# Moving the output spectra between two vector engines in a cross-attention and FFN kernel

## The reference

```python
q, k, v = LN(x) @ Wq.T + bq, ctx @ Wk.T + bk, ctx @ Wv.T + bv     # (4, 512, 16, 16)
corr = irfft(rfft(q) * conj(rfft(k))).mean(channels)              # (4, 16, 512)
weights, delays = top_k(corr, 6); w = softmax(weights)
out = sum_i w[i] * roll(v, delays[i]);  x = x + out @ Wo.T + bo
h = gelu(bitlinear(LN(x), w1, b1))                                # (4, 512, 1024)
x = x + bitlinear(h, w2, b2)
# bitlinear(x, w, b): y = rmsnorm(x); scale = 127 / max|y| per row; round(y * scale) / scale,
#                     w rounded to -1, 0, 1 times mean|w|; then a matrix product and the bias
```

## Time and profile before

| what | us |
|---|---|
| median of 3 runs | 181.0 |
| lowest and highest run | 180.97, 183.41 |
| the profiled execution | 182.84 |
| its span, first to last instruction | 180.8 |
| busy: TensorE, ScalarE, GpSimd | 159.7, 89.7, 83.9 |
| mean granted TensorE clock over the span, as a share of full speed | 0.98 |

### The profile page before, as it was taken

How to read it: one execution, slowest core, us unless ns; L and a number is a source line. 1 busy time by engine, 2 the same in 40 slices (tenths; PEclk the granted TensorE clock), 3 DMA queues, 4 the chain that set the end, 5 groups by cost and what they waited for, 6 DMA issues and landing times.

```text
span 180.8 us, 2886 instructions
## 1 busy us (share of the span) xinstructions
PE 159.7 (88%) x869; PEld 107.1 (59%) x877; DVE 149.8 (83%) x347; ACT 89.7 (50%) x158; POOL 83.9 (46%) x150
## 2 busy tenths in 40 slices
PE   7989889998999998999994977993799999999943
PEld 2635667657655956576873755670456766555632
DVE  1537299999299996999979999779997999999992
ACT  3136615548722441211510521519449999999821
POOL 6030899754440003932009827071985654454430
PEclk9999999999999999999999999999589999999999
DMA  5999989080474000000000001616447101111012
GB/s 191 319 289 391 359 289 190 3 116 0 64 107 61 5 0 0 0 0 5 2 0 0 0 0 29 91 29 87 64 59 115 58 29 58 44 45 62 29 58 87
DMA packets 14128, 15.07 MB, mean 83 GB/s; under 512 B 1186, under 2 KB 13347, under 8 KB 14116
## 3 DMA queue, kind: packets, MB, share of 16 engines
q1 hardware_dynamic: 9892, 10.73, 17.9%
q0 software_dynamic: 4224, 4.19, 15.8%
HBM read 8.61 MB, written 2.10 MB: 59 GB/s over the span
## 4 chain that ended last, share of the span: by engine, by line
PE 25%; DVE 24%; issue 7%; POOL 1%; DVEq 1%; ACT 0%; POOLq 0%
PE psum L469 4%; PE psum L458 4%; DVE c_f L1046 4%; PE psum L518 4%; PE psum L538 3%; DVE res L1061 2%; DVE hmax L1035 2%; DVE stats L910 2%; PE psum L520 2%; PE psum L338 2%; PE psum L529 2%; DVE prod_sum L763 1%; DVE xmax L924 1%; DVE m_b L884 1%; DVE out_f L891 1%
## 5 line engine op out<-in xcount | busy, mean ns | idle before, releaser
L390 PE MATMUL psum<-wkv,c_f 128*128 128x512 f32 x64 | 29.0, 598 | 0.8 <-ACT c_f L580 0.8
L1035 DVE TENSOR_REDUCE hmax<-wf 128x1 f32<-128x1025 f32 x16 | 19.4, 1211 | 0.7 <-ACT wf L683 0.7
L390 PEld LDWEIGHTS psum<-wkv,c_f 128*128 128x128 f32 x64 | 11.8, 190 | 13.7 <-issue 12.4
L683 ACT ACTIVATE wf<-psum,xdeq 128x1024 f32<-128x1024 f32 x16 | 17.6, 1101 | 1.3 <-PE psum L520 1.3
L599 ACT COPY kv_f<-psum 128x512 f32<-128x512 f32 x16 | 9.1, 582 | 18.4 <-PE psum L390 18.4
L691 ACT ACTIVATE x_f<-wf 128x1024 f32<-128x1024 f32 x16 | 16.9, 1056 | 0.0
L458 PE MATMUL psum<-to_signal,out_f 128*128 128x256 f32 x64 | 14.6, 382 | 2.4 <-POOL out_f L1170 2.4
L518 PE MATMUL psum<-w1q,xq_t 128*128 128x512 bf16 x59 | 16.2, 392 | 0.5 <-issue 0.3
L538 PE MATMUL psum<-w2q,kv_f 128*128 128x256 bf16 x128 | 16.4, 273 | 0.0
L469 PE MATMUL psum<-wo,out_t 128*128 128x256 f32 x64 | 14.9, 386 | 1.3 <-DVE out_t L898 1.3
L403 PE MATMUL psum<-wq,x_f 128*128 128x256 f32 x64 | 15.1, 381 | 0.8 <-ACT x_f L580 0.8
(11 more groups left out here) (164 smaller groups left out, 351.0 us busy)
## 6 DMA issues: line engine op xcount, KB each, us to landing
ctx_in<-in_ctx SPq DMA_DIRECT2D x4, 512.0 KB, 5.1
res<-in_x SPq DMA_DIRECT2D x4, 512.0 KB, 6.5
res<-bo_all POOLq DMA_DIRECT2D x4, 512.0 KB, 5.2
res<-b_all POOLq DMA_DIRECT2D x4, 512.0 KB, 5.9
out<-res SPq DMA_DIRECT2D x16, 128.0 KB, 1.7
wf<-in_w_t SPq DMA_DIRECT2D x1, 1024.0 KB, 8.3
wf<-in_w_t SPq DMA_DIRECT2D x2, 512.0 KB, 9.7
wkv<-in_wkv_t SPq DMA_DIRECT2D x1, 512.0 KB, 7.5
```

The lines of the kernel that those rows point to most:

```text
L390: mm = pe.matmul(bank(K_BANKS + ft), c_f[:, c, ft * P:(ft + 1) * P], wkv[:, c, :], start=(c == 0), stop=(c == NC - 1))
L683: act.activation(hid[j], hb, ACT.Gelu, scale=xdeq[:, m, j:j + 1]).then_inc(s["hid_made"], 1)
L1035: dve.tensor_reduce(hmax[:, j:j + 1], hid_and_least[j], AX.X, ALU.max, apply_absolute_value=True).then_inc(s["hmax_made"], 1)
```

## The change

- **Output spectra by batch.** GpSimd computes real and imaginary part of batches 0, 1 and 3 (`out_spectrum`, six instructions of 128x512 each, in place of three for every batch). VectorE computes batch 2 in two halves of heads (`out_spectrum_halves`, twelve instructions of 128x256), and TensorE may start half c = 0 once the first six are done. `out_f` becomes a pair of buffers.
- **Weights of the delays.** The comparison that made a mask (L835) goes; one instruction selects and sums; the scaling of a 32x512 tile becomes that of a 32x32 diagonal, by which TensorE's turn multiplies.
- **Rounding of x** goes from VectorE to ScalarE (`round_x`, four activations); VectorE gets a small multiplication for the scale (`x_scales`) and keeps the cast (`whole_x`).
- **PSUM banks.** Projection uses banks 4 and 5, the turns of x 2 and 3 (for batches 2 and 3: 6 and 7).
- **TensorE's order.** `up(0, 0)` goes between the halves of `inverse(3)`; the turns of batches 2 and 3 go to tiles 4 and 6.
- **Late norms between tiles.** On VectorE the residual, norm and maximum of batches 2 and 3 are spread over tiles 0 to 4, and ScalarE's and GpSimd's orders follow.

```diff
-                    pe.wait_ge(s["out_im_made"], n + 1)
+                if n == FIRST_LATE:
+                    pe.wait_ge(s["out_half_made"], 2 * c + 2)
+                elif c == 0:
...
             pe.wait_ge(s["consts"], 3)
-            for n in (2, 3):
-                inverse(n, 0)
-                inverse(n, 1)
-                keep_busy(M_BANKS[1], 5)
-                project(n, 0)
-                project(n, 1)
-                turn_x(n - 2)
 
             def up(m, j):
...
 
+            inverse(2, 0)
+            inverse(2, 1)
+            keep_busy(X_BANKS, 5)
+            project(2, 0)
+            project(2, 1)
+            turn_x(0)
+            inverse(3, 0)
             pe.wait_ge(s["w_quantised"], 2)
             pe.wait_ge(s["b1_made"], 16 * NPART)
+            up(0, 0)
+            inverse(3, 1)
+            keep_busy(X_BANKS, 5)
+            project(3, 0)
+            project(3, 1)
+            turn_x(1)
+            pe.wait_ge(s["xt_copied"], 4)
             for m in (0, 1):
                 for j in range(NA):
                     t = NA * m + j
+                    for n in X_TURNED:
+                        if t == X_TURNED[n] + 1:
+                            pe.wait_ge(s["xt_copied"], n * 2 + 2)
                     if t > TURNED:
                         turn_h(m, j)
-                    if t == 1:
-                        pe.wait_ge(s["at_used"], 4 * NB)
-                    up(m, j)
-                    if t == 1:
-                        turn_x(2)
+                    if t:
+                        up(m, j)
                     if t == 2:
...
 
+            def round_x(n):
+                act.wait_ge(s["xscale_made"], n + 1)
+                if n:
+                    act.wait_ge(s["xq_made"], n)
+                for a in range(NA):
+                    ins = act.activation(xround[:, a, :], xc[:, n % 2, a, :], ACT.Identity, scale=xscale[:, a:a + 1])
+                ins.then_inc(s["xround"], 1)
+
             def copy_x(n):
...
+            inverse_copy(3, 0)
+            gelu(0, 0)
+            inverse_copy(3, 1)
+            square(0, 0)
+            round_x(1)
+            centre(2)
+            copy_x(1)
             for m in (0, 1):
...
+                    for n in X_TURNED:
+                        if t == X_TURNED[n]:
+                            copy_x(n)
                     if t >= COPIED:
                         copy_h(m, j)
-                    if t == 0:
+                    if t:
+                        square(m, j)
+                    if t == 2:
                         centre(3)
-                    if t == 1:
-                        copy_x(2)
-                    square(m, j)
...
+            def weigh(g):
+
                 dve.wait_ge(s["rest_made"], g + 1)
-                dve.tensor_tensor(rest[:, 0:L], corr[:, 0:L], rest[:, 0:L], ALU.not_equal).then_inc(s["mask_made"], 1)
-
-            def weigh(g):
-
-                dve.wait_ge(s["mask_made"], g + 1)
                 dve.wait_ge(s["exp_made"], g + 1)
-                dve.tensor_tensor_reduce(out=expd[:], in0=expd[:], in1=rest[:, 0:L], scale=1.0, scalar=0.0,
-                                         op0=ALU.mult, op1=ALU.add, accum_out=gsum[:]).then_inc(s["gsum_made"], 1)
+                dve.scalar_tensor_tensor(chosen[:], rest[:, 0:L], TAKEN, expd[:], ALU.is_le, ALU.mult,
+                                         accum_out=gsum[:]).then_inc(s["gsum_made"], 1)
                 dve.wait_ge(s["gsum_made"], g + 1)
                 dve.reciprocal(grec[:], gsum[:]).then_inc(s["grec_made"], 1)
                 dve.wait_ge(s["grec_made"], g + 1)
-                dve.tensor_scalar(chosen[:], expd[:], grec[:, 0:1], None, ALU.mult).then_inc(s["g_made"], 1)
+                dve.tensor_scalar(g_diag[:], eye[0:GR, 0:GR], grec[:, 0:1], None, ALU.mult).then_inc(s["g_made"], 1)
...
+            def out_spectrum_halves(n):
+                dve.wait_ge(s["g_ready"], n // (NB // NG) * 3 + 3)
+                dve.wait_ge(s["at_done"], n * 4 - 6)
+                v = [by_heads(kv_f[:, n, part:part + 3:2, D:2 * D]) for part in range(2)]
+                g_r, g_i, g_x = [g[:, :, bass.ds(n * H, H)].unsqueeze(3).broadcast_to([P, 2, H, DK]) for g in (g_re, g_im, g_rx)]
+                m = [by_heads(m_halves[:, k]) for k in range(4)]
+                for c in range(NC):
+                    h = slice(c * H // NC, (c + 1) * H // NC)
+                    cols = slice(c * P, (c + 1) * P)
+                    dve.tensor_tensor(m[0][:, :, h], v[0][:, :, h], g_r[:, :, h], ALU.mult)
+                    dve.tensor_tensor(m[1][:, :, h], v[1][:, :, h], g_i[:, :, h], ALU.mult).then_inc(s["m_half_made"], 1)
+                    dve.tensor_tensor(m[2][:, :, h], v[1][:, :, h], g_x[:, :, h], ALU.mult)
+                    dve.tensor_tensor(m[3][:, :, h], v[0][:, :, h], g_i[:, :, h], ALU.mult).then_inc(s["m_half_made"], 1)
+                    dve.wait_ge(s["m_half_made"], 2 * c + 1)
+                    dve.tensor_tensor(out_f[:, n % 2, :, 0, cols], m_halves[:, 0, :, cols], m_halves[:, 1, :, cols],
+                                      ALU.subtract).then_inc(s["out_half_made"], 1)
+                    dve.wait_ge(s["m_half_made"], 2 * c + 2)
+                    dve.tensor_tensor(out_f[:, n % 2, :, 1, cols], m_halves[:, 2, :, cols], m_halves[:, 3, :, cols],
+                                      ALU.add).then_inc(s["out_half_made"], 1)
 
             def inverse_out(n, c):
...
             copy_g_spectrum(1)
-            out_re_products(2)
-            out_re(2)
+            out_spectrum_halves(FIRST_LATE)
...
                 inverse_out(n, 1)
-                if n + 1 < NB:
-                    out_re_products(n + 1)
-                    out_re(n + 1)
-                quantise_x(n - 2)
                 x_deq(n - 2)
-            add_residual(3, 0)
-            add_residual(3, 1)
-            stats2(3)
-            mean_var2(3)
-            row_max(2)
-            x_inverse(2)
-            quantise_x(2)
-            x_deq(2)
-
+                whole_x(n - 2)
...
-                    if (m, j) == (0, 0):
+                    if t == 0:
+                        add_residual(3, 0)
+                        add_residual(3, 1)
+                        row_max(2)
+                        x_scales(2)
+                        x_deq(2)
+                    if t == 1:
+                        stats2(3)
+                        mean_var2(3)
+                        whole_x(2)
+                    if t == 2:
                         row_max(3)
-                        x_inverse(3)
-                        quantise_x(3)
+                        x_scales(3)
                         x_deq(3)
+                    if t == 4:
+                        whole_x(3)
...
+                    pool.wait_ge(s["out_re_made"], by_pool(n) - 1)
+                    pool.wait_ge(s["out_im_made"], by_pool(n) - 1)
+                pool.tensor_tensor(by_heads(m_a[:]), v_of(n, 0), g_of(g_re, n), ALU.mult)
+                pool.tensor_tensor(by_heads(m_b[:]), v_of(n, 1), g_of(g_im, n), ALU.mult).then_inc(s["m_ab"], 1)
                 pool.tensor_tensor(by_heads(m_c[:]), v_of(n, 1), g_of(g_rx, n), ALU.mult)
                 pool.tensor_tensor(by_heads(m_d[:]), v_of(n, 0), g_of(g_im, n), ALU.mult).then_inc(s["m_cd"], 1)
-
-            def out_im(n):
-
-                pool.wait_ge(s["m_cd"], n + 1)
-                if n:
-                    pool.wait_ge(s["at_done"], n * 4 - 2)
-                pool.tensor_tensor(out_f[:, :, 1, :], m_c[:], m_d[:], ALU.add).then_inc(s["out_im_made"], 1)
+                if n > 1:
+                    pool.wait_ge(s["at_done"], n * 4 - 6)
+                pool.wait_ge(s["m_ab"], by_pool(n))
+                pool.tensor_tensor(out_f[:, n % 2, :, 0, :], m_a[:], m_b[:], ALU.subtract).then_inc(s["out_re_made"], 1)
+                pool.wait_ge(s["m_cd"], by_pool(n))
...
-            for n in (0, 1):
-                out_im_products(n)
-                out_im(n)
-            out_im_products(2)
-            out_im(2)
+            out_spectrum(0)
+            out_spectrum(1)
+            out_spectrum(3)
             x_rms(0)
-            out_im_products(3)
-            out_im(3)
             aug_parts(0)
             add_b2(0)
             x_rms(1)
             aug_parts(1)
             add_b2(1)
```

More of the change, by code:

```diff
@@ L1234, in _ @@
             add_b2(2)
+            h_deq(0, 1)
             x_rms(3)
[L1236 removed]
+            h_deq(0, 2)
+            add_b2(3)
+            h_deq(0, 3)
+            h_deq(1, 0)
             aug_parts(3)
[L1238 to L1242 removed]
+            for j in range(1, NA):
+                h_deq(1, j)
             with pool.Fori(2, NB) as m:
```

121 lines of the change are left out of this document (54 added, 67 removed).

## The result

The changed kernel takes **194.45 us** (median of 4, 192.32 to 195.92) against 181.45 of the kernel before on the same chip (lowest and highest 180.97 and 183.41): ratio 1.0615, 95% interval 1.0462 to 1.0769. That is slower, as forecast, but by 13 in place of 7.5 and outside the range. The profiled execution took 195.21. Page: span, and busy time by engine, against the earlier trace rows.

A forecast was written before the change was run, and what follows sets the result against it. Busy shares named no bound; TensorE's path was taken as longest up to T0, VectorE as pacing after it. Shifts of 2.2 and 5.3 on the 181.0 median gave 188.5 us, range 180 to 191.

The forecast's parts named there:

- Order of the work by turns: At the memory ports VectorE and GpSimd alternate; each waits for one whole instruction of the other, however short its own.
- Part 1: First group's spectra: cross spectra wait for GpSimd by turns, `correlate(1)` at about 84.0 instead of 81.77, T0 2.2 later.
- Part 1 and 2: Turns at the cross spectra, then at batch 2's halves beside batch 3: halves ready about 7.0 and 10.1 after T0.
- T0: Moment the second weights' spectrum is ready, 94.51 before the change; forecast to come 2.2 later.
- TensorE gains the 0.5 that it waited there: Before the first weights' spectrum: without GpSimd's bias row in VectorE's way, the spectrum is ready at 71.2 instead of 71.7.
- all unchanged: TensorE from `correlate(1)` to the second weights' spectrum: projection, inverse, turn and spectrum keep their lengths.
- Part 3: VectorE from T0 to tile 3: 40.7 of work plus 7.9 of waits, 48.6 in place of 43.3, 5.3 later.
- From there on its order per tile is untouched by the change, but for one cast of 0.3, so what follows keeps its length: VectorE from the hidden maximum of tile 3 (137.85 before) to the end: no change in length forecast.
- The moved turns of batches 2 and 3 lie behind VectorE's pace: TensorE's later turns of x: claimed not to hold VectorE up, so no time was added for them.
- VectorE keeping the ports, wholly or in part: Ports: GpSimd's turn comes only at the end (177.8, chance 0.16), or VectorE gets two turns for one (about 181, 0.14).
- That the clock costs nothing: Projection of batch 2: the clock holds or recovers in time, VectorE's wait shrinks by 2.6, giving 185.8; chance 0.20.
- Rivals 1 and 4: Clock costs nothing (185.8, chance 0.20); clock also falls before `correlate(1)`, costing TensorE up to 2.6 (190.9, chance 0.08).

The follow-up runs named there:

- b1: Kernel before with only the new output spectra by batch (batch 2 in halves on VectorE, the rest on GpSimd, pair of buffers): 190.42 us, ratio 1.0430.
- b4: Changed kernel with the split of the spectra undone (real parts on VectorE, imaginary on GpSimd, one buffer): 185.4 us, ratio 1.0184.
- x4: Changed kernel with 17 more unread matmuls before the third inverse and 16 more before batch 2's projection: 193.31 us, ratio 1.0626.
- d2: Kernel before, batch 2 halved on VectorE, GpSimd's batch 3 after it, idle matmuls before batch 2's projection (17) and turn (16): 180.08 us, ratio 0.9886.
- c1: Kernel before with a pair of buffers, batch 2 in halves on VectorE and batch 3 on GpSimd only after them: 182.97 us, ratio 1.0046.
- x1: Changed kernel with GpSimd's batch 1 held until the cross spectra are made and batch 3 until the halves are: 188.7 us, ratio 1.0331.
- e2: Changed kernel with late turns mended (banks, GpSimd's bias row, VectorE's cast) and GpSimd held behind cross spectra and halves: 184.58 us, ratio 1.0193.
- x2: Changed kernel with ScalarE's rounding of batch 3 moved behind the copy of batch 2's turn in tile 4: 192.38 us, ratio 1.0540.
- x3: Changed kernel with batch 2 turned at tile 3 in the projection's banks: 195.05 us, no ratio given.
- d3: Changed kernel, spectra split undone, batch 2 turned at tile 3 in projection banks, GpSimd's bias parts and VectorE's cast of batch 3 earlier: 182.18 us, ratio 0.9991.
- e3: Changed kernel, late turns mended, GpSimd held behind cross spectra and halves, unread matmuls added before (17) and behind (16) the third inverse: 184.96 us, ratio 1.0205.
- d1: Kernel before with 16 idle matmuls ahead of the turn of batch 2: 182.19 us, ratio 0.9976.
- e1: Changed kernel with late turns mended: batch 2 turned at tile 3 in projection banks, GpSimd's last bias row and VectorE's last cast earlier: 191.76 us, ratio 1.0523.

## Why the prediction was wrong

- **Order of the work by turns** (how the engines meet; Part 1 and 2): right. The cross spectra took 0.30, 1.09, 0.93 and 1.30 (the first came only 0.2 before a GpSimd instruction ended), `correlate(1)` came at 84.06 for a forecast of 84.0, the sixth instruction of the halves ended 6.6 and the twelfth 9.7 after T0 for 7.0 and 10.1. The hit at 84.0 is in part luck: the four instructions took 3.5 for a forecast of 3.9, and the first weights' spectrum was ready at 71.8 for 71.2. b1's +2.2 from A to B is what the split costs there; Part 1 had 2.7 for it (2.2 for T0 and 0.5 for the earlier A). The Trainium skill (SBUF — State Buffer, section "SBUF: two separate sides") gives the exclusion, and the trace agrees (1.28 for work of 0.34). It names no order of turns; the alternation is what these rows add.
- **"TensorE gains the 0.5 that it waited there"; turn and spectrum "all unchanged"** (Part 1): wrong. I read the new diagonal as a smaller tile for VectorE to scale and did not price the turn itself, which goes from 0.43 to 1.07. It is paid twice. In the first group it eats the 0.5 (A moved by 0.06), in the second it adds 0.64; b4 has exactly that, 23.44 for 22.80.
- **Part 3**: 47.3 from T0 to tile 3 for 48.6, since waits came to 6.9 of the 7.9. The projection started 17.4 after T0 for a forecast of 17.8, in a low clock as forecast, and took 5.41 for 6.1. The clock's share in VectorE's waits shows in the traces: 1.7 in x4, 2.4 in d2 against c1, 1.4 between x1 and e2. In the times only d2 shows it. Its share in the waits behind tile 3 is not shown by a run.
- **The step that failed**: "From there on its order per tile is untouched by the change, but for one cast of 0.3, so what follows keeps its length", and with it "The moved turns of batches 2 and 3 lie behind VectorE's pace". Priced at 0, measured +5.5. (The cast of 0.3 was taken off B to C and added nowhere.) VectorE's order was indeed untouched; what fed it was not. I had moved a turn to a tile and never followed the banks it was moved into: banks 6 and 7 are those of `turn_h`, so the copy on ScalarE became a condition for the next tile's transposes, with 2.8 of other ScalarE work ahead of it. b4 shows it without the split, b1 shows it absent with the split, x2, x3 and x1 leave it in place wholly or mostly, and d3 and e2 take 3.3 and more of it away by mending that chain alone. 1.7 of it remains in the mended versions, and how the rest divides between the banks and the half clock behind the gap is an estimate only.
- **Rivals.** VectorE keeping the ports, wholly or in part, is refuted by the rows of the halves. That the clock costs nothing is refuted by the projection's 5.41 in the change against 3.72 in x4, with VectorE's waits for it at 3.9 and 2.2. Rivals 1 and 4 add up to 185.9 and 191.1 from their own terms, not 185.8 and 190.9; nothing hangs on it. A fall of the clock in Part 1 did not occur: 1.77 of gap ahead of `correlate(1)`, and 1.91 long behind it as before.

Forecast terms 2.2 + 5.3 + 0 against 2.9 + 4.0 + 5.5. That the first two come to 6.9 for 7.5 is luck, since one was 0.7 too low and the other 1.3 too high. Not separated by any run: which of the rounding on ScalarE, the late norms and `up(0, 0)` inside the inverse earns b4's 3.2; and what the spectra of batches 0 and 1 on GpSimd alone cost (A to B in e2 is still 24.17, 0.7 above b4). Of this 0.7, x1's trace has 0.4 at `correlate(1)`, behind a first inverse that starts 6.9 after A in place of 5.9, and 0.3 at the second inverse, for which GpSimd, held back by x1's own wait, is ready only at 86.7. The three edits of d3's mend are not separated either, but that the turn at tile 3 alone (x3) gained nothing.

## What to carry to other kernels

When an instruction is moved, follow its output buffer as well as its engine: who writes there next, and what stands ahead of the read that frees it. Work split over VectorE and GpSimd by instruction count is priced in turns, not in sums; a short VectorE instruction beside GpSimd costs a GpSimd instruction, so keep the critical short ones out of such stretches with a wait. A stage made ready early only pays if TensorE's next gap is filled too (c1 against d2), and filling beyond the gap costs what it saves (e3).

## What was not expected of the hardware

- A gap of TensorE of about the same length ended in either clock. Before the third inverse, 2.42 was followed by 3.69 in the kernel before; in d1, the same gap was followed by 5.38:

```profile
99.91 5.38 PE L458 MATMUL psum<-to_signal,out_f 128*128 128x256 f32 x16 [2.42 <-POOL out_f L1171]
```

The clock over 99 to 105 was 0.72 in d1 and 1.00 before, and d1's edit comes into play only behind 120. b4 and d3 are such a pair too: 2.39 of gap, then 5.38 and 3.69. In x3 and e1 the clock fell between 94 and 96, though TensorE had no gap over 0.2 since 83. Executions of one kernel therefore differ in how often the clock falls, which may be why the kernel before ranges from 180.72 to 184.57 over these groups (mean clocks 1.00 and 0.97 in these two) and x3 from 189.53 to 195.29.
- What a half clock costs depends on who waits behind it. Ahead of the third inverse it cost VectorE next to nothing: d3 and b4 differ by 1.7 in that row and by 0.1 in B to C. At the projection it cost all of it: x1 and e2 differ by 1.4 in both.
- At T0 the first of the halves started 0.05 ahead of GpSimd and took 0.43, hardly more than alone, while GpSimd's took 1.30 for 1.06 alone. The turns began with VectorE's second.
